# S4 with its two terms multiplied one by one and added in PSUM, for the first three sub-tiles

## The chip, the cores and the metric

The kernel runs on one core of a Trainium2 chip. The metric is the time of one execution on the device, in microseconds (us): the median of several runs.

## What is computed

The reference takes `x` of shape (32, 128, 64, 2): for each of 32 channels and 128 heads a row of 64 complex coefficients. Cut to what matters:

```python
dtA = (-exp(inv_A_real) + 1j * A_imag) * exp(log_dt)[:, None]     # (128 heads, 64)
Cc = B * C * (exp(dtA) - 1.0) / A
V = exp(dtA[:, :, None] * arange(1024))
h = 2.0 * einsum('chn,hnl->chl', Cc, V).real                      # S4: (32, 128, 1024)
h = h + einsum('bsi,oi->bso', layernorm(h), attn_weight) + attn_bias
n = layernorm(h)
gates = softmax(n @ Wr.T)
h = h + n @ W.T + b + sum_e 2.0 * gates[e] * (n @ A[e].T) @ Bm[e].T
```

So an S4 kernel matrix is built for each (channel, head), which gives 4096 tokens of 1024 values, and two 1024 x 1024 layers with a layer norm each follow; the second has a gated low-rank part.

## The kernel before, in words

The 4096 tokens are worked on in 32 sub-tiles of 128 tokens (4 heads of 32 channels). Two sub-tiles, i = 0 and 1, make a tile T (8 heads); there are 16 tiles. J = 2 * T + i numbers the sub-tiles.

**S4.** A position on the 1024 steps is split into a block a (8 of them, `KB`) and a step b (128). The real part over 64 complex coefficients is a contraction over 128 rows: 64 real and 64 imaginary. `make_u` (VectorE) multiplies `decay` by the sines in `turn` and gives `u`, a 128 x 128 matrix per head over the steps b. `make_m` (VectorE) gives the other operand, `m`, per head 8 blocks of 32 channels. It has two terms, because a complex product has two products: `x_t` part 0 times `q1` goes to `m`, `x_t` part 1 times `q2` goes to `m_im` (both L998), and the third instruction (L1001) adds `m_im` to `m`. All three are 128 x 1024 in fp32. `s4` (TensorE, L441) then takes for each block a and head q one product: `m[:, i, q, a*32:(a+1)*32]` is stationary (32 columns), `u` of the head is moving (128 columns), and the result goes to the 32 partitions q*32 of `ps_a`, columns a*128. The four heads of a block stand on the four column groups of the array. That is 32 products in each sub-tile; each shows as two matmuls and two weight loads in the profile.

**Behind S4.** `keep_h` (VectorE, L1007) reads `ps_a` when S4 is done, adds the bias into `h_tok` and sums for the mean; `square_1` (ScalarE, L683) sums the squares; `normalise_1` (VectorE, L1016 to L1032) makes `y` from `ps_a`; `high_1` (ScalarE, L703) and `low_1` (VectorE, L1038) split it into two fp16 halves in `x1_tok`, and SP's queue sends each through a DMA transpose (`turn_x1`). `attn` (TensorE, L449) takes 48 matmuls of 512 columns. `keep_h2` (VectorE, L1046), `square_2`, `normalise_2`, `high_2`, `low_2` and `turn_x2` do the same for the second layer; `project` (L497, L499) is its low-rank part and gate, `ffn_part` (L509) and `ffn_end` (L520) the layer, `finish` (L1108) the last addition.

**The prologue.** Ahead of the loop over the tiles the kernel also makes `q1`, `q2`, the first `u`, and turns and splits both weight matrices: the attention weight through TensorE (`turn_weight`, L487), then ScalarE (`wa_hi`, L728) and VectorE (`wa_lo`, L1149); the FFN weight through ScalarE (L739), VectorE (L1157) and DMA transposes (`turn_weights`). All of it is woven with the first three sub-tiles, (0,0), (0,1) and (1,0). The fourth, (1,1), is the first in the loop.

**What sets the order.** Each engine has its own list of calls, written out by hand, and runs it in that order; semaphores tie the lists together. For the change these matter: `s_terms` counts the two terms of `make_m`, `s_m` its sums, `s_s4` the finished S4 products, `s_h2` the `keep_h2`. `make_m` of the next sub-tile overwrites `m_im`. TensorE's list around the first two S4 is

```python
            turn_weight(1)
            pe.wait_ge(s_q, 2)
            s4(0, 0)
            square_ffn(KB + 2, KB + 4)
...
            attn_part(0, 0, range(0, 4), (0,))
            s4(0, 1)
            pe.wait_ge(s_wlo, low_done(5))
            turn_weight(7)
```

and for the third `ffn_part(0, 0, range(0, 3), (0,))` stands ahead of `s4(1, 0)`. On VectorE `make_m(0, 0)` is followed by `make_first_u(0)`, then `keep_h(0, 0)`, `attn_lo(0, 1)` and `normalise_1(0, 0)`; `make_m(0, 1)` by `attn_lo(5)`, `ffn_lo(8)`, `attn_lo(6)`, `keep_h(0, 1)`, `attn_lo(7)`; `make_m(1, 0)` by `keep_h2(0, 1)`, `make_u(1)`, the gate of (0,0) and `keep_h(1, 0)`.

Of the kernel before, what the change touches and what calls it, by code (L numbers as in the profile page):

```python
# [15 lines left out]
P = 128  # L16
C, H, N = 32, 128, 64
# [9 lines left out]
HS = P // C  # L27
# [21 lines left out]
BELOW_PI = 3.1415925  # L49
BELOW_TWO_PI = 6.283185  # L50
NA = KB + 2
PRE = EXPS + 40


def at_least(engine, semaphore, value):

    if isinstance(value, int) and value <= 0:
        return
    engine.wait_ge(semaphore, value)


def program(nc, x, log_dt, B, inv_A_real, A_imag, attn_w, attn_b, ffn_w, ffn_b, lora_a, lora_b,
            gate_w, out):
    with ExitStack() as ctx:
# [14 lines left out]
        steps_b = sb("steps_b", [P, P])  # L79
        steps_a = sb("steps_a", [P, NA])  # L80
        half_pi = sb("half_pi", [P, 1])
# [20 lines left out]
        m = sb("m", [P, SUB, HS, KB * C])  # L102
        m_im = sb("m_im", [P, HS, KB * C])
# [22 lines left out]
        turn, u = turn_u[:, 0, :, :], turn_u[:, 1, :, :]  # L126
# [14 lines left out]
        ps_a = ctx.enter_context(nc.psum_tensor("ps_a", [P, 2, HALF], F32))  # L141
# [48 lines left out]
        s_terms = sem("m_terms_ready")  # L190
        s_m = sem("m_ready")
        s_s4 = sem("s4_product_done")
# [72 lines left out]
        def scratch(where, *shape):  # L265
# [23 lines left out]
        ga, gb = scratch("y", 2, N), scratch("y", 2, N)  # L289
        ph, ph_k = scratch("x1_tok", NA, N), scratch("x1", NA, N)  # L290
        sc = turn_u[:, :, :, :].rearrange("p s a b -> p s (a b)")[:, :, 0:NA * N]\
            .rearrange("p s (a n) -> p s a n", n=N)
# [24 lines left out]
        def _(sp):  # L317
# [58 lines left out]
            for n in range(KB, 2 * KB):  # L376
                sp.dma_start(raw_block(n), ffn_rows[n - KB]).then_inc(s_wload[n], 16)
            sp.wait_ge(s_pre_dve, PRE)
            load_lora_a(wg_norm_rows, s_wgn)
# [39 lines left out]
        def _(pe):  # L419
# [11 lines left out]
            def s4(T, i):  # L431

                if isinstance(T, int) and (T, i) == (0, 0):
                    pe.wait_ge(s_u_0, 1)
                else:
                    pe.wait_ge(s_u, T + 1)
                pe.wait_ge(s_m, 2 * T + i + 1)
                at_least(pe, s_xn1, 2 * T + i)
                for a in range(KB):
                    for q in range(HS):  # L440
                        mm = pe.matmul(ps_a[q * C:(q + 1) * C, a // 4, (a % 4) * P:(a % 4 + 1) * P],  # L441
                                       m[:, i, q, a * C:(a + 1) * C], u[:, HS * i + q, :], start=True, stop=True)
                mm.then_inc(s_s4, 1)

            def attn_part(t, i, ks, halves=(0, 1), ps=ps_g1):
# [102 lines left out]
            pe.wait_ge(s_pre_act, 6)  # L548
            for first, dst, ready in ((0, ps_g1, PRE - 1), (N, ps_a, PRE)):
                pe.wait_ge(s_pre_dve, ready)  # L550
                for a in range(KB):
                    mm = pe.transpose(dst[:, a // 4, (a % 4) * P:(a % 4 + 1) * P], qn[:, a, first:first + 2 * N],
                                      ident[:, :])
# [78 lines left out]
            for o in range(2):  # L632
                cols = slice(o * HALF, (o + 1) * HALF)
                for k in range(KB):
                    if (o, k) == (0, 6):
                        turn_lora(t, 1)
                    for part, ws in ((0, wf_hi), (0, wf_lo), (1, wf_hi)):
                        pe.matmul(ps_g1[:, o, :], x2_part(1, part)[:, k, :], ws[:, k, cols],  # L638
                                  start=k == 0 and part == 0 and ws is wf_hi, stop=False)
# [211 lines left out]
        def _(pool):  # L851
# [3 lines left out]
                               pattern=[[-1, P]], channel_multiplier=1).then_inc(s_const, 1)  # L855
            pool.iota(steps_a[:, 2:NA], pattern=[[P, KB]], base=0, channel_multiplier=0,
                      allow_small_or_imprecise_dtypes=True).then_inc(s_const, 1)
# [13 lines left out]
        def _(dve):  # L871
# [11 lines left out]
            for tile, value in ((ones[:, :], 1.0), (half_pi[:, :], pi / 2), (quarter[0:N, :], 0.25),  # L883
                                (quarter[N:P, :], 0.0), (eps[:, :], EPS), (steps_a[:, 0:1], 0.5),
                                (steps_a[:, 1:2], 1.0)):
                last = dve.memset(tile, value)
# [11 lines left out]
            for k in range(6, 0, -1):  # L898
# [17 lines left out]
            tt(wexp, zr[:, 0:1, :].broadcast_to((P, KB, N)),  # L916
               steps_a[:, 2:NA].unsqueeze(2).broadcast_to((P, KB, N)), ALU.mult)
            tt(ph, zt[:, 0:1, :].broadcast_to((P, NA, N)), steps_a[:, :].unsqueeze(2).broadcast_to((P, NA, N)),
               ALU.mult)
# [38 lines left out]
            tt(qn[:, :, 2 * N:3 * N], wb[:, 1, :, :], wa[:, 0, :, :], ALU.subtract)  # L958
            assert done[0] == PRE

# [23 lines left out]
            def make_m(T, i):  # L984

                J = 2 * T + i
                dve.wait_ge(s_xt_sb, T + 1)
                at_least(dve, s_s4, J - 1)
                if isinstance(T, int):
                    at_least(dve, s_m, J)  # L990
                for part, dst in enumerate((m[:, i, :, :], m_im[:, :, :])):
                    c = x_t[:, part, i * P:(i + 1) * P].rearrange("p (h c) -> p h c", h=HS)\
                        .unsqueeze(2).broadcast_to((P, HS, KB, C))
                    f = (q1, q2)[part][:, :, columns(T, i)].rearrange("p a h -> p h a")\
                        .unsqueeze(3).broadcast_to((P, HS, KB, C))
                    if isinstance(T, int) and J == 0:
                        dve.wait_ge(s_q, part + 1)
                    dve.tensor_tensor(dst.rearrange("p h (a c) -> p h a c", a=KB), c, f, ALU.mult)\  # L998
                        .then_inc(s_terms, 1)
                dve.wait_ge(s_terms, 2 * J + 2)  # L1000
                dve.tensor_tensor(m[:, i, :, :], m[:, i, :, :], m_im[:, :, :], ALU.add).then_inc(s_m, 1)  # L1001

# [181 lines left out]
            round_turns(0)  # L1184
            dve.wait_ge(s_pre_dve, PRE)
            weight_norms(0, [whole(ps_g2)])
# [114 lines left out]
```

## Time and profile before

| | before |
|---|---|
| median of 3 runs | 840.18 us |
| lowest and highest | 838.75 and 841.95 us |
| the profiled execution, its own time | 838.85 us |
| its span, first to last instruction | 837.0 us |
| TensorE matmul busy | 811.0 us (97%) |
| VectorE busy | 586.9 us (70%) |
| ScalarE busy | 376.6 us (45%) |
| mean granted TensorE clock | 0.993 |

The profile is of one execution. Engines are PE (TensorE matmul), PEld (TensorE weight load), DVE (VectorE), ACT (ScalarE), POOL and SP (queues of DMA issues); L441 is line 441 of the kernel. Times are in us from the start of the span. "Idle before" is the time the engine did nothing ahead of an instruction, with what released it. The granted clock is 1.00 for 2.4 GHz and 0.50 for 1.2 GHz. The records of pipelined matmuls overlap: the busy time of a group is the time covered by at least one.

### The profile page before, as it was taken

How to read it: one execution, taken by the hardware profiler on the slowest of the kernel's cores; microseconds unless marked ns; L12 is line 12 of the kernel's file. 1: busy time of each engine (PE TensorE's matmuls, PEld its weight loads, DVE VectorE, ACT ScalarE, POOL GpSimd, SP SyncE). 2: the span in 40 equal slices, each digit the busy share in tenths (PEclk: the TensorE clock that was granted, in tenths of full speed). 3: DMA queues.
4: the chain of work that ended last, by engine and by line, in shares of the span. 5: the costliest groups of instructions: out<-in, count | busy, mean ns of one | idle time of the engine just before them, and what ended most of it. 6: DMA issues, size and time to landing. Idle time of an engine off the chain costs nothing.

```text
span 837.0 us, 16105 instructions
## 1 busy us (share of the span) xinstructions
PE 811.0 (97%) x6098; PEld 431.0 (51%) x6098; DVE 586.9 (70%) x1150; ACT 376.6 (45%) x747; POOL 3.0 (0%) x10
## 2 busy tenths in 40 slices
PE   6978799999999999999999999999999999999998
PEld 6854345545554555555545554555455555544543
DVE  6989786776758777675767677676867667577533
ACT  4767652625444352545445253545435254442210
POOL 0000000000000000000000000000000000000000
PEclk9999999999999999999999999999999999999999
DMA  7637644234323332333232323332233233323223
GB/s 267 193 71 136 131 88 77 67 71 87 75 51 73 65 87 52 86 76 76 62 75 63 75 63 75 84 78 51 65 74 83 55 88 75 71 54 67 59 51 76
DMA packets 175267, 68.47 MB, mean 82 GB/s; under 512 B 160456, under 2 KB 168776, under 8 KB 175248
## 3 DMA queue, kind: packets, MB, share of 16 engines
q1 hardware_dynamic: 175152, 68.09, 36.7%
q8 instruction: 11, 0.18, 0.1%
q10 hardware_dynamic: 96, 0.13, 0.0%
q14 instruction: 8, 0.07, 0.0%
HBM read 13.67 MB, written 16.78 MB: 36 GB/s over the span
## 4 chain that ended last, share of the span: by engine, by line
PE 88%; DVE 5%; issue 3%; ACT 2%; DMA 1%; SPq 0%; POOL 0%; POOLq 0%; ACTq 0%; DVEq 0%
PE ps_g L509 38%; PE ps_g L449 38%; PE ps_a L441 7%; PE ps_g L520 2%; PE ps_g L638 1%; PE ps_p L497 1%; PE ps_g L463 1%; PE ps_x L427 1%; DMA h_tok<-in_L_attn_weight 1%; PE ps_p L499 1%; DVE m L998 0%; DVE m_im L998 0%; PE ps_p L514 0%; ACT phase L657 0%; DVE wa_lo L1149 0%
## 5 line engine op out<-in xcount | busy, mean ns | idle before, releaser
L449 PE MATMUL ps_g<-wa_hi,x 128*128 128x512 f16 x1024 | 271.5, 381 | 2.9 <-DMA x<-x_tok 2.2
L509 PE MATMUL ps_g<-wf_hi,x 128*128 128x512 f16 x992 | 265.7, 381 | 1.1 <-DVE h_tok L1046 1.1
L449 PEld LDWEIGHTS ps_g<-wa_hi,x 128*128 128x128 f16 x1024 | 97.7, 98 | 123.4 <-issue 7.4
L449 PE MATMUL ps_g<-wa_lo,x 128*128 128x512 f16 x512 | 154.4, 381 | 0.0
L509 PEld LDWEIGHTS ps_g<-wf_hi,x 128*128 128x128 f16 x992 | 94.9, 98 | 108.0 <-issue 2.8
L509 PE MATMUL ps_g<-wf_lo,x 128*128 128x512 f16 x496 | 149.6, 381 | 0.0
L683 ACT ACTIVATE junk<-ps_a,stat 128x1024 bf16<-128x1024 f32 x32 | 35.6, 1113 | 147.4 <-DVE stat L1010 147.4
L1108 DVE SCALAR_TENSOR_TENSOR result<-ps_g,unscale,h_tok 128x1024 f32<-128x1024 f32 x31 | 39.8, 1283 | 72.0 <-PE ps_g L520 72.0
L703 ACT ACTIVATE x_tok<-y 128x1024 f16<-128x1024 f32 x32 | 33.8, 1057 | 123.4 <-DVE y L1032 123.4
L449 PEld LDWEIGHTS ps_g<-wa_lo,x 128*128 128x128 f16 x512 | 50.2, 98 | 60.7 <-issue 1.0
L509 PEld LDWEIGHTS ps_g<-wf_lo,x 128*128 128x128 f16 x496 | 48.5, 98 | 58.6 <-issue 0.6
L689 ACT ACTIVATE junk<-h_tok,stat 128x1024 bf16<-128x1024 f32 x32 | 36.7, 1147 | 91.0 <-DVE stat L1050 91.0
L441 PE MATMUL ps_a<-turn_u,m 128*32 128x128 f32 x2048 | 62.5, 274 | 2.4 <-DVE m L1001 2.1
L441 PEld LDWEIGHTS ps_a<-turn_u,m 128*32 128x32 f32 x2048 | 54.0, 110 | 10.8 <-issue 9.2
L1007 DVE SCALAR_TENSOR_TENSOR h_tok<-ps_a,bias_bc 128x1024 f32<-128x1024 f32 x32 | 39.2, 1223 | 24.7 <-PE ps_a L441 24.7
L1046 DVE SCALAR_TENSOR_TENSOR h_tok<-ps_g,unscale,h_tok 128x1024 f32<-128x1024 f32 x32 | 41.0, 1281 | 20.7 <-PE ps_g L449 20.7
L1038 DVE TENSOR_TENSOR x_tok<-y,x_tok 128x1024 f16<-128x1024 f32 x32 | 39.1, 1222 | 21.3 <-ACT x_tok L703 21.3
L709 ACT ACTIVATE stage<-xn 128x1024 f16<-128x1024 f32 x32 | 33.8, 1056 | 44.6 <-DVE xn L1057 44.6
L657 ACT ACTIVATE phase<-steps_b,quarter,z_turn 128x128 f32<-128x128 f32 x128 | 50.8, 479 | 0.0
L1063 DVE TENSOR_TENSOR stage<-xn,stage 128x1024 f16<-128x1024 f32 x32 | 39.2, 1225 | 11.4 <-ACT stage L709 11.4
L1032 DVE TENSOR_SCALAR y<-ps_a,stat 128x1024 f32<-128x1024 f32 x32 | 43.0, 1343 | 1.2
L998 DVE TENSOR_TENSOR m<-x_t,q 128x1024 f32<-128x1024 f32 x32 | 39.2, 1224 | 1.6
(188 smaller groups left out, 782.4 us busy)
## 6 DMA issues: line engine op xcount, KB each, us to landing
out<-result SPq DMA_DIRECT2D x124, 128.0 KB, 2.1
x_raw<-in_x SPq DMA_DIRECT2D x64, 64.0 KB
stage<-in_L_ffn_W SPq DMA_DIRECT2D x8, 512.0 KB, 9.8
h_tok<-in_L_attn_weight SPq DMA_DIRECT2D x2, 512.0 KB, 4.8
x<-in_L_attn_weight SPq DMA_DIRECT2D x2, 512.0 KB, 7.2
result<-in_L_attn_weight SPq DMA_DIRECT2D x2, 512.0 KB, 8.7
x<-x_tok SPq DMA_TRANSPOSE x64, 3.2
x<-stage SPq DMA_TRANSPOSE x64, 3.2
```

The source lines that it names most:

```text
L441: mm = pe.matmul(ps_a[q * C:(q + 1) * C, a // 4, (a % 4) * P:(a % 4 + 1) * P], m[:, i, q, a * C:(a + 1) * C], u[:, HS * i + q, :], start=T ...
L449: mm = pe.matmul(ps[:, o, :], x1_part(part, ps is ps_g2)[:, k, :], ws[:, k, o * HALF:(o + 1) * HALF], start=k == 0 and part == 0 and ws is ...
L509: pe.matmul(ps_g2[:, o, :], xs[:, k, :], ws[:, k, o * HALF:(o + 1) * HALF], start=k == 0 and xs is x2_hi and ws is wf_hi, stop=False)
L657: a = act.activation(phase[:, k, :], steps_b[:, :], ACT.Identity, scale=z_turn[:, bass.ds(T * HT + k, 1)], bias=quarter[:, :])
L689: act.activation(junk[:, :], h2_tok[:, i, :], ACT.Square, bias=stat_2[:, 1:2], accum_out=stat_2[:, 2:3]).then_inc(s_ssq2, 1)
L998: dve.tensor_tensor(dst.rearrange("p h (a c) -> p h a c", a=KB), c, f, ALU.mult)\
L1007: dve.scalar_tensor_tensor(out=h_tok[:, i, :], in0=whole(ps_a), scalar=1.0, in1=bias_bc[:, :], op0=ALU.mult, op1=ALU.add, accum_out=stat_1 ...
L1032: dve.tensor_scalar(y[:, :], whole(ps_a), stat_1[:, 1:2], stat_1[:, 7:8], ALU.add, ALU.mult).then_inc(s_xn1, 1)
L1038: dve.tensor_tensor(by_token(x1_tok[:, :], 1), y[:, :], by_token(x1_tok[:, :], 0), ALU.subtract)\
L1046: dve.scalar_tensor_tensor(out=h2_tok[:, i, :], in0=whole(ps), scalar=unscale[:, 0:1], in1=h_tok[:, i, :], op0=ALU.mult, op1=ALU.add, accu ...
L1063: dve.tensor_tensor(by_token(x2_tok, 1), xn[:, :], by_token(x2_tok, 0), ALU.subtract)\
L1108: dve.scalar_tensor_tensor(out=result[:, i, :], in0=whole(ps_g2), scalar=unscale[:, 1:2], in1=h2_tok[:, i, :], op0=ALU.mult, op1=ALU.add). ...
```

## The change

For J below `APART` = 3, `make_m` ends behind its two terms. `s4` waits for both (`s_terms`) and multiplies each with `u`: for each block a the four products with `m` (start of the PSUM group), then the four with `m_im` (its end). For all other sub-tiles nothing changes but the count in the waits on `s_m`, which has three sums fewer.

```diff
+APART = 3
@@ s4 (TensorE)
-                pe.wait_ge(s_m, 2 * T + i + 1)
+                if isinstance(T, int) and 2 * T + i < APART:
+                    pe.wait_ge(s_terms, 2 * (2 * T + i) + 2)
+                else:
+                    pe.wait_ge(s_m, 2 * T + i + 1 - APART)
                 at_least(pe, s_xn1, 2 * T + i)
+                terms = (m[:, i, :, :], m_im[:, :, :]) if isinstance(T, int) and 2 * T + i < APART else (m[:, i, :, :],)
                 for a in range(KB):
-                    for q in range(HS):
-                        mm = pe.matmul(ps_a[q * C:(q + 1) * C, a // 4, (a % 4) * P:(a % 4 + 1) * P],
-                                       m[:, i, q, a * C:(a + 1) * C], u[:, HS * i + q, :], start=True, stop=True)
+                    for term, last in zip(terms, (len(terms) == 1, True)):
+                        for q in range(HS):
+                            mm = pe.matmul(ps_a[q * C:(q + 1) * C, a // 4, (a % 4) * P:(a % 4 + 1) * P],
+                                           term[:, q, a * C:(a + 1) * C], u[:, HS * i + q, :],
+                                           start=term is terms[0], stop=last)
@@ make_m (VectorE)
                 if isinstance(T, int):
-                    at_least(dve, s_m, J)
+                    at_least(dve, s_m, J - APART)
+                    at_least(dve, s_s4, min(J, APART))
...
+                if isinstance(T, int) and 2 * T + i < APART:
+                    return
                 dve.wait_ge(s_terms, 2 * J + 2)
                 dve.tensor_tensor(m[:, i, :, :], m[:, i, :, :], m_im[:, :, :], ALU.add).then_inc(s_m, 1)
```

How the order of instructions changes is shown at two places. On TensorE, around the S4 of sub-tile (0,0), before (L487 is `turn_weight(1)`, L463 the squares of the FFN weight):

```order
L487 MATMUL ps_g<-ident,h_tok 128x128 x8
L441 MATMUL ps_a<-turn_u,m 32x128 x32
L463 MATMUL ps_x<-stage 128x128 x4
L463 MATMUL ps_p<-stage 128x128 x4
L463 MATMUL ps_x<-stage 128x128 x4
```

and with the change, whose lines are numbered 6 or 7 higher here (the pair of L447 rows stands eight times in all):

```order
L494 MATMUL ps_g<-ident,h_tok 128x128 x8
L447 MATMUL ps_a<-turn_u,m 32x128 x4
L447 MATMUL ps_a<-turn_u,m_im 32x128 x4
L447 MATMUL ps_a<-turn_u,m 32x128 x4
L447 MATMUL ps_a<-turn_u,m_im 32x128 x4
```

One row of 32 products has become 16 rows of 4, 64 products in all; the same stands at (0,1) and (1,0).

On VectorE, from `make_m(1, 0)` on, before (with the semaphores waited for):

```order
L998 TENSOR_TENSOR m<-x_t,q 128x1024 [waits m_ready,s4_product_done,x_transposed_copied]
L998 TENSOR_TENSOR m_im<-x_t,q 128x1024
L1001 TENSOR_TENSOR m<-m,m_im 128x1024 [waits m_terms_ready]
L1046 SCALAR_TENSOR_TENSOR h_tok,stat<-ps_g,unscale,h_tok 128x1024 [waits attn_product_done,first_ffn_rows_transposed]
L1050 TENSOR_SCALAR stat<-stat 128x1 [waits h2_ready]
```

and with the change:

```order
L1006 TENSOR_TENSOR m<-x_t,q 128x1024 [waits s4_product_done,x_transposed_copied]
L1006 TENSOR_TENSOR m_im<-x_t,q 128x1024
L1056 SCALAR_TENSOR_TENSOR h_tok,stat<-ps_g,unscale,h_tok 128x1024 [waits attn_product_done,first_ffn_rows_transposed]
L1060 TENSOR_SCALAR stat<-stat 128x1 [waits h2_ready]
L981 TENSOR_TENSOR turn_u<-decay,turn_u 128x1024 [waits s4_product_done,decay_ready,sines_ready]
```

The sum is gone, and `keep_h2(0, 1)` follows the second term directly. No other instruction moves on any engine, and SP's queue is the same.

## Rows read from the trace of the kernel before

**Rows 1.** The page, part 1, busy time of each engine.

```profile
PE 811.0 (97%) x6098; PEld 431.0 (51%) x6098; DVE 586.9 (70%) x1150; ACT 376.6 (45%) x747; POOL 3.0 (0%) x10
```

**Rows 2.** TensorE's waits from 105 us to the end.

```profile
PE ps_a L441 <- DVE m L1001: 2.1, 1, 2.1
```

**Rows 3.** The chain that ended last, 88 to 118 us: start, us, what.

```profile
88.07 3.74 PE ps_g L509 x9
...
105.37 1.95 PE ps_a L441 x64
107.32 10.47 PE ps_g L449 x48
```

**Rows 4.** Windows: stretch, its length, busy (instructions) of PE, PEld, DVE, ACT, POOL, granted clock, DMA, GB/s.

```profile
44.00:47.20 3.20, 0.00 (x0) 0.00 (x0) 3.20 (x4) 3.11 (x5) 0.00 (x0) 0.97 0.71 137
...
68.60:70.70 2.10, 0.00 (x0) 0.00 (x0) 2.02 (x2) 2.05 (x2) 0.00 (x0) 1.00 0.98 190
71.20:74.00 2.80, 2.80 (x8) 0.89 (x6) 2.73 (x10) 2.80 (x9) 0.00 (x0) 0.50 0.99 190
83.90:86.20 2.30, 0.00 (x0) 0.00 (x0) 2.27 (x3) 2.28 (x6) 0.00 (x0) 1.00 0.99 190
88.00:91.20 3.20, 3.13 (x8) 1.20 (x9) 2.08 (x7) 2.98 (x7) 0.00 (x0) 0.50 0.96 185
...
103.40:105.20 1.80, 0.00 (x0) 0.00 (x0) 1.76 (x3) 1.80 (x6) 0.00 (x0) 1.00 1.02 193
```

**Rows 5.** Timeline, first sub-tile: start, us, engine, line, operation.

```profile
32.41 1.23 DVE L1001 TENSOR_TENSOR m<-m,m_im 128x1024 f32<-128x1024 f32 x1
...
33.00 1.03 PE L487 MATMUL ps_g<-ident,h_tok 128*128 128x128 f32 x8
33.56 0.68 DVE L981 TENSOR_TENSOR turn_u<-decay,turn_u 128x512 f32<-128x512 f32 x1
...
34.34 1.95 PE L441 MATMUL ps_a<-turn_u,m 128*32 128x128 f32 x64 [0.31 <-issue]
...
36.42 1.22 DVE L1007 SCALAR_TENSOR_TENSOR h_tok<-ps_a,bias_bc 128x1024 f32<-128x1024 f32 x1 [0.58 <-PE ps_a L441]
```

**Rows 6.** The page, part 5, the S4 products and their loads.

```profile
L441 PE MATMUL ps_a<-turn_u,m 128*32 128x128 f32 x2048 | 62.5, 274 | 2.4 <-DVE m L1001 2.1
L441 PEld LDWEIGHTS ps_a<-turn_u,m 128*32 128x32 f32 x2048 | 54.0, 110 | 10.8 <-issue 9.2
```

**Rows 7.** Timeline, second sub-tile: start, us, engine, line, operation [idle before].

```profile
54.45 1.22 DVE L1001 TENSOR_TENSOR m<-m,m_im 128x1024 f32<-128x1024 f32 x1
...
55.83 1.96 PE L441 MATMUL ps_a<-turn_u,m 128*32 128x128 f32 x64
...
58.90 0.69 ACT L728 ACTIVATE wa_hi<-ps_x,scale 128x512 f16<-128x512 f32 x1 [3.35 <-PE ps_p L487]
...
59.31 1.21 DVE L1007 SCALAR_TENSOR_TENSOR h_tok<-ps_a,bias_bc 128x1024 f32<-128x1024 f32 x1
59.49 0.68 ACT L728 ACTIVATE wa_hi<-ps_p,scale 128x512 f16<-128x512 f32 x1
...
60.87 1.11 ACT L683 ACTIVATE junk<-ps_a,stat 128x1024 bf16<-128x1024 f32 x1 [0.70 <-DVE stat L1010]
```

**Rows 8.** Timeline, third sub-tile.

```profile
85.50 1.23 DVE L1001 TENSOR_TENSOR m<-m,m_im 128x1024 f32<-128x1024 f32 x1
...
86.50 1.06 ACT L677 ACTIVATE turn_u<-turn_u 128x1024 f32<-128x1024 f32 x1
...
86.64 1.28 DVE L1046 SCALAR_TENSOR_TENSOR h_tok<-ps_g,unscale,h_tok 128x1024 f32<-128x1024 f32 x1
...
86.75 0.18 PE L499 MATMUL ps_p<-wg,x 128*128 128x36 f16 x1
...
88.07 0.59 PE L509 MATMUL ps_g<-wf_hi,x 128*128 128x512 f16 x1 [1.14 <-DVE h_tok L1046]
...
93.76 1.23 DVE L1007 SCALAR_TENSOR_TENSOR h_tok<-ps_a,bias_bc 128x1024 f32<-128x1024 f32 x1 [1.77 <-PE ps_a L441]
```

## The prediction

> **What bounds the kernel now.** I read the page's busy shares first: TensorE is busy for 97% of the span, VectorE for 70% [rows 1]. A share over the whole span says little about a change that touches the first 105 us alone, so the next view is TensorE's waits. From 105 us to the end there is one, of 2.1 us, before S4 of the fourth sub-tile, for VectorE's sum of its `m` [rows 2]. Behind that product TensorE never waits again. So the kernel has two parts. From 105.37 us on [rows 3] it is a fixed stretch of TensorE work, and all before is a prologue whose length is the start of that S4. **What the change is worth is the shift of this one start.**
>
> In the prologue neither engine works alone. VectorE runs nearly without a break and feeds TensorE; TensorE stands idle in gaps (the windows show four without one matmul) [rows 4]. But at three places VectorE waits for TensorE, and these are the three S4 products of the change, because `keep_h` reads `ps_a` when S4 is done.
>
> **The price of one product and of one sum.** S4 of a sub-tile is 32 products, recorded as 64 matmuls, and takes 1.95 us [rows 5]. One matmul's record lasts 274 ns [rows 6], but four products run side by side on four column groups, so they follow each other every 30.5 ns. The second term adds 64 records: I take **+1.95 us for each of the three sub-tiles**. The sum that VectorE saves lasts 1.23 us and frees it 1.15 us earlier (32.41 to the next start, 33.56) [rows 5].
>
> The stationary operand is loaded twice as often, too. The 2048 loads last 110 ns each but take 54.0 us together [rows 6], 1.7 us for the 64 of a sub-tile, inside the products' 1.95. The Trainium skill speaks against this change here: "TensorE: Matmul & The Clock Gate", section Part 3 on packing small matmuls, has loads overlap matmuls in flight only where the row group differs, and here all loads use all 128 rows. By that rule the 64 added loads would lie bare, an estimate of 7 us for each sub-tile, and the sum below would come to about 19 us. The trace disagrees, and it decides.
>
> **First sub-tile (0,0).** TensorE ends `turn_weight(1)` at 34.03 and starts S4 at 34.34, released by `u`, which VectorE ends at 34.24 behind the sum [rows 5]. Without the sum `u` is there at 33.1, and TensorE itself is next: S4 starts 0.3 us earlier and ends 1.95 - 0.3 = 1.65 us later. `keep_h` (36.42) had waited for it already, so it goes 1.65 us later. Behind it on VectorE stand the `wa_lo` splits, `normalise_1` and `low_1`, behind S4 on TensorE the squares and `turn_weight(2)`; each feeds the other, and both are late by the same amount. VectorE then runs on without a long wait to the second sub-tile. **+1.6 us.**
>
> **Second sub-tile (0,1).** The sum ends at 55.67 and S4 starts at 55.83, straight behind TensorE's attention piece: its row shows no idle time ahead [rows 7]. So S4 gains nothing from the missing sum: the engine was not free. VectorE gets its three weight splits done 1.15 us sooner, and then waits in `keep_h` (59.31 before) for an S4 that ends 1.95 us later: `keep_h` itself goes some 0.55 us later. The larger delay runs past it. `turn_weight(7)` (L487) stands behind S4, ScalarE's two halves of `wa_hi` (58.90 to 60.17) wait for it, and `square_1` (60.87) stands behind them on ScalarE [rows 7]. They now end at 62.12, so `square_1`, with the whole normalisation, is 1.25 us later. **+1.2 us.**
>
> **Third sub-tile (1,0).** VectorE comes to it with no slack and goes from the sum (85.50) straight to `keep_h2` (86.64), for which TensorE's FFN piece waits until 88.07 [rows 8]. Without the sum that is 1.15 us sooner; the projection that ends at 86.93 (last matmul 86.75) then releases it, at about 86.95. So FFN and S4 start 1.1 us sooner. `make_u` must be ready: the sine it needs ends at 87.56, `u` then at 88.9, before the end of the FFN piece at 88.07 + 3.74 - 1.1 = 90.7 [rows 3]. S4 ends 1.95 - 1.1 = 0.85 us later, and `keep_h` (93.76), for which VectorE had already idled 1.77 us [rows 8], follows. From there to the fourth `m` it is a chain through `keep_h`, both normalisations and `low_1`. **+0.85 us.**
>
> SP's queue issues its transposes when the splits are ready, so they move with them; no DMA is added. The added semaphore waits cost nothing: for `m_im` VectorE waits for an S4 whose result its own `keep_h` has already waited for. The loop's code issues as many instructions as before. **Sum: 1.6 + 1.2 + 0.85 = +3.65 us.**
>
> **The clock** is the unknown term. TensorE is granted 0.50 (1.2 GHz) from 88.0 to 91.2, after two gaps in which it did almost nothing (2.3 us from 83.9, 1.1 us from 86.93 with the short projection between them) [rows 4, 8]. The nine FFN matmuls before the third S4 take 3.74 us there, where the 48 of the loop's attention take 10.47, or 0.218 us each [rows 3]; so the low level costs 3.74 - 1.96 = 1.8 us on the path. The change closes the second gap and leaves one of about 2.4 us. A gap of 2.1 us from 68.6 was followed by 0.50, one of 1.8 to 2.1 us before 105.37 was not [rows 4]. The bounds are -1.8 (the low stretch is gone) and +1.8 (another falls on the path, on a doubled S4, say). I take -0.5: the nearest rows say one and the other, and what is saved early can be lost again to another wait. **Total +3.15 us.** The profiled execution took 838.85 us, so it would take 842.0; the median of the runs, 840.18, is 1.33 above it, and the forecast is **843.3 us**, +0.37%, which is no change within the 0.5% (4.2 us) that a measurement of this kernel can tell.
>
> **Rival 1: the clock comes back.** The shortened gap no longer ends in the low level. The Trainium skill, same page, section Part 1 on the clock gate, states that activity releases the throttle and idle time brings it, which would favour this case. By rows it is 3.65 - 1.8 = +1.85, 842.0 us. For it: the second gap vanishes. Against it: the gap of 2.1 us at 68.6 fell.
>
> **Rival 2: the products hide.** TensorE has idle time in the prologue (gaps of 3.2, 2.1, 2.3 and 1.8 us) [rows 4], and if the second term lay in it, only VectorE's gains would be left: 0.3 at the first sub-tile, 0.7 at the second (`square_1` would follow `wa_hi` at 60.2 instead of 60.87) [rows 7], 1.1 at the third, about -2 in all and 838.2 us, still inside 0.5%. Against it: VectorE waits for S4 in two of three `keep_h`, with 0.58 and 1.77 us of idle time [rows 5, 8].
>
> **Rival 3: slower.** The two terms of one slice add into the same columns of `ps_a`, eight records or 0.24 us apart, while one record lasts 0.27 us. If the second must wait for the first to be through, S4 takes longer than twice 1.95 us. It decides from 0.35 us per sub-tile on (3 x 0.35 + 3.15 = 4.2). A stall of 0.06 us in each of 8 slices is 0.5 us, 1.5 in all: 844.8 us. With a further low stretch on the path it would be up to 846.6. Against it: the attention matmuls add into the same columns one straight after the other and keep their pace of 0.218 us at 0.38 us per record.
>
> **Rival 4: it does not do what it says.** The built program has the 64 products and no sum in exactly three places, so I leave this 1%.
>
> **Chances.** My sum with the low stretch in place 43%, rival 1 33%, rival 2 11%, rival 3 12%, rival 4 1%. Over 4.2 us slower come most of rival 3 and a quarter of the first case, whose 843.8 lies 0.5 below the limit: 20%. Faster than 836.0 is only a good run of rival 2 with the clock gained as well: 4%. The same: 76%. The range goes from rival 1 less the spread of the runs shown (838.75 to 841.95, so 1.5 to 1.8 on each side), 840.2, to rival 3 with half of its further low stretch, 845.9.
>
> **What the new profile would show.** S4 of the first three sub-tiles as 128 matmuls in 3.9 us; `keep_h` 1.6 us later at 38.1; `wa_hi` of block 7 near 62.5 (58.90 before); `keep_h2` of (0,1) near 88.4; the fourth S4 near 108.5, with TensorE waiting for the sum ahead of it and for nothing after it. I am wrong if a 128-record S4 lasts much over 3.9 us, if the shift at the fourth S4 isn't the shift of the end, or if the fourth S4 starts no later than 105.4.

## The result, and the profile after

| | before | with the change |
|---|---|---|
| median | 839.77 us (22 runs) | 841.87 us (22 runs) |
| lowest and highest | 836.33 and 841.95 us | 839.99 and 843.22 us |
| the profiled execution, its own time | 838.85 us | 842.04 us |
| its span | 837.0 us | 840.2 us |
| mean granted TensorE clock | 0.993 | 0.994 |

The ratio of the times is **1.0025, with a 95% interval of 1.0013 to 1.0036**: 2.1 us slower, which is no change within 0.5%. The forecast was 843.3 us and no change. Each kernel's runs spread over 3 to 6 us, more than the effect, so only many runs show its sign.

The page of the changed kernel, part 1, against [rows 1]:

```profile
PE 815.2 (97%) x6290; PEld 435.9 (52%) x6290; DVE 583.5 (69%) x1147; ACT 376.6 (45%) x747; POOL 3.0 (0%) x10
```

TensorE has 192 matmuls more and 4.2 us more busy time. VectorE has three instructions and 3.4 us less. The page's part 5, the S4 products with `m` and their loads, against [rows 6]:

```profile
L447 PE MATMUL ps_a<-turn_u,m 128*32 128x128 f32 x2048 | 66.4, 274 | 2.1 <-DVE m L1011 2.1
...
L447 PEld LDWEIGHTS ps_a<-turn_u,m 128*32 128x32 f32 x2048 | 54.4, 110 | 10.7 <-issue 9.1
```

TensorE's waits from 105 us to the end, as in [rows 2]: still one, of the same length, ahead of the fourth S4. The loop behind it is the same stretch as before.

```profile
PE ps_a L447 <- DVE m L1011: 2.1, 1, 2.1
```

The chain that ended last, 50 to 118 us (start, us, what), against [rows 3]:

```profile
52.38 1.97 PE ps_g L494 x8
54.35 3.36 PE ps_g L456 x12
57.71 3.63 PE ps_a L447 x128
...
89.08 0.19 PE ps_p L504
89.69 3.57 PE ps_g L516 x9
93.27 3.72 PE ps_a L447 x128
97.01 1.24 DVE h_tok L1017 x2
...
107.26 1.24 DVE m L1011
...
108.62 1.95 PE ps_a L447 x64
```

The second S4 and the third now take 3.63 and 3.72 us for 128 records, and both stand on the chain. The fourth S4 starts at 108.62 instead of 105.37, 3.25 us later, and the profiled execution is 3.19 us longer: the shift of this one start is the shift of the end.

Windows of the same trace (stretch, length, busy time and instructions of PE, PEld, DVE, ACT, POOL, granted clock, DMA, GB/s), against [rows 4]:

```profile
49.40:55.40 6.00, 4.81 (x19) 3.54 (x19) 5.62 (x11) 4.37 (x5) 0.72 (x1) 0.50 0.23 58
...
85.10:88.90 3.80, 0.00 (x0) 0.00 (x0) 3.80 (x5) 3.78 (x11) 0.00 (x0) 1.00 0.91 173
90.20:93.00 2.80, 2.80 (x8) 0.79 (x6) 1.89 (x5) 2.74 (x5) 0.00 (x0) 0.50 0.97 187
```

The two stretches in the low level both lie on the path here: one on the transposes of the attention weight and the attention products ahead of the second S4, one on the FFN products ahead of the third. The gap ahead of the FFN products has become one long one, 4.18 us up to the projection at 89.08.

Timeline of the changed kernel at the three places (start, us, engine, line, operation [idle before]), against [rows 5, 7, 8]:

```profile
31.65 0.68 DVE L988 TENSOR_TENSOR turn_u<-decay,turn_u 128x512 f32<-128x512 f32 x1
...
33.32 0.43 PE L447 MATMUL ps_a<-turn_u,m 128*32 128x128 f32 x8
...
33.56 0.40 PE L447 MATMUL ps_a<-turn_u,m_im 128*32 128x128 f32 x8
...
33.78 0.40 PE L447 MATMUL ps_a<-turn_u,m 128*32 128x128 f32 x8
...
37.16 1.22 DVE L1017 SCALAR_TENSOR_TENSOR h_tok<-ps_a,bias_bc 128x1024 f32<-128x1024 f32 x1 [3.22 <-PE ps_a L447]
...
61.41 1.23 DVE L1017 SCALAR_TENSOR_TENSOR h_tok<-ps_a,bias_bc 128x1024 f32<-128x1024 f32 x1 [3.11 <-PE ps_a L447]
...
63.62 1.11 ACT L690 ACTIVATE junk<-ps_a,stat 128x1024 bf16<-128x1024 f32 x1
...
87.00 1.22 DVE L1006 TENSOR_TENSOR m_im<-x_t,q 128x1024 f32<-128x1024 f32 x1
88.14 1.28 DVE L1056 SCALAR_TENSOR_TENSOR h_tok<-ps_g,unscale,h_tok 128x1024 f32<-128x1024 f32 x1
...
97.01 1.22 DVE L1017 SCALAR_TENSOR_TENSOR h_tok<-ps_a,bias_bc 128x1024 f32<-128x1024 f32 x1 [2.26 <-PE ps_a L447]
```

Eight records start every 0.22 us, whichever term they multiply. And where the sum stood, VectorE now waits: 3.22, 3.11 and 2.26 us ahead of the three `keep_h`, against 0.58, none and 1.77.

**How the shift grows.** The first `m` of a run starts between 28.5 and 30.0 us, with nothing of the change ahead of it (30.02 before, the latest of all traces, and 29.38 here). So I compare starts counted from it. The columns of the experiments below are read in the same way.

| start of | before | change | terms ×2, sums kept | no sums, one term |
|---|---|---|---|---|
| `keep_h` (0,0) | 36.42 | +1.38 | +1.75 | -0.36 |
| S4 (0,1) | 55.83 | +2.45 | +1.75 | +0.93 |
| `y` (0,1) | 63.60 | +3.39 | +2.69 | +0.13 |
| `keep_h2` (0,1) | 86.64 | +2.14 | +2.70 | -1.12 |
| FFN piece | 88.07 | +2.14 | +2.71 | -1.12 |
| `keep_h` (1,0) | 93.76 | +3.89 | +5.43 | -1.71 |
| fourth S4 | 105.37 | +3.89 | +5.43 | -1.71 |

In the change's column +1.38 is the first place. From +1.38 to +2.45 nothing of the change is at work: the 12 attention products ahead of the second S4 run in the low level and take 3.36 us, where the second kernel of the table takes 2.59. From S4 to `y` it is +0.94, the second place. Then -1.25 (the sum), +1.75 (the product) and -0.05 (the FFN products, which take 3.70 us from their first start at 89.57 instead of 3.74) make +0.5 at the third. **The three places cost 1.38 + 0.94 + 0.5 = 2.8 us, and the clock 1.1, against this one execution of the kernel before.**

The split hangs on that execution. Its low stretch there, 47.1 to 50.5 us, ended ahead of the attention products, so its second S4 came early. Three of the runs below have the lists of before up to that place: (1,0) alone, the unused products at the projection, and `keep_h2` moved alone. In all three a low stretch reaches into the attention products, and the second S4 starts 1.3, 2.0 and 1.1 us later than in the table's column. From S4 to `y` they take 6.97 us instead of 7.77. Here are S4 and `y` before, 7.77 us apart, and then in the run with unused products, 6.97 apart:

```profile
55.83 1.96 PE L441 MATMUL ps_a<-turn_u,m 128*32 128x128 f32 x64
63.60 1.34 DVE L1032 TENSOR_SCALAR y<-ps_a,stat 128x1024 f32<-128x1024 f32 x1
```

```profile
57.17 1.95 PE L441 MATMUL ps_a<-turn_u,m 128*32 128x128 f32 x64
64.14 1.34 DVE L1035 TENSOR_SCALAR y<-ps_a,stat 128x1024 f32<-128x1024 f32 x1
```

The change takes 8.71. So against an execution whose S4 is late too, the second product costs its full 1.74 us and the three places 3.6 in all. The `y` of those three runs is 0.3, 1.2 and 0.5 us later than before's (`keep_h2` alone, unused products, (1,0) alone), so against them the shift at `y` is 2.2 to 3.1 us instead of 3.39, and nothing of it is left for the clock.

### The profile page after: what moved, and what is told of

Read it like the earlier page. It is cut to its first block, busy times and chain, and to the rows that moved or that the text cites. A ratio compares the mean times of both kernels' runs of the same rounds, so it can differ in the third digit from the quotient of the medians.

```text
span 840.2 us, 16486 instructions
## 1 busy us (share of the span) xinstructions
PE 815.2 (97%) x6290; PEld 435.9 (52%) x6290; DVE 583.5 (69%) x1147; ACT 376.6 (45%) x747; POOL 3.0 (0%) x10
## 4 chain that ended last, share of the span: by engine, by line
PE 89%; DVE 5%; issue 3%; ACT 1%; DMA 1%; SPq 0%; POOL 0%; POOLq 0%; DVEq 0%; ACTq 0%
PE ps_g L456 38%; PE ps_g L516 37%; PE ps_a L447 7%; PE ps_g L527 2%; PE ps_g L645 1%; PE ps_p L504 1%; DVE params L885 1%; PE ps_x L428 1%; PE ps_p L506 1%; PE ps_p L521 0%; DMA x<-stage 0%; DVE y L885 0%; ACT phase L664 0%; DVE h_tok L885 0%; DMA params<-in_L_tok_B 0%
## 5 line engine op out<-in xcount | busy, mean ns | idle before, releaser
L447 PE MATMUL ps_a<-turn_u,m 128*32 128x128 f32 x2048 | 66.4, 274 | 2.1 <-DVE m L1011 2.1
L447 PEld LDWEIGHTS ps_a<-turn_u,m 128*32 128x32 f32 x2048 | 54.4, 110 | 10.7 <-issue 9.1
```

## Experiments

### The second product and the missing sum, each alone

With the sums kept (`make_m` is that of before), each product of the first three S4 is written twice; the lines are shown against the change's `s4`:

```diff
-                terms = (m[:, i, :, :], m_im[:, :, :]) if isinstance(T, int) and 2 * T + i < APART else (m[:, i, :, :],)
+                terms = (m[:, i, :, :],) * (2 if isinstance(T, int) and 2 * T + i < APART else 1)
...
-                                           start=term is terms[0], stop=last)
+                                           start=True, stop=True)
```

> The three sums stay on VectorE, and TensorE writes each of the 32 products of the first three S4 twice, to the same place (64 products, same result). Theory A (S4 is bare on the path at all three places, a second term costs 1.7 us each as the changed kernel's trace has it: 3.65 instead of 1.9 us): the fourth S4 starts about 5.2 us later against the prologue's own start than before, and the time is about 845 us, 0.6% over before. Rival B (the added products lie largely in TensorE's idle time and the change's loss has another cause): less than 1.5 us over before.

And the change with its sums left out, but its products with the first term alone, so that the second term's part of S4 is missing:

```diff
-                terms = (m[:, i, :, :], m_im[:, :, :]) if isinstance(T, int) and 2 * T + i < APART else (m[:, i, :, :],)
+                terms = (m[:, i, :, :],)
```

> The sums are left out, and S4 of the first three sub-tiles multiplies the first term only, 32 products (the second term's part of S4 is missing there, so the time is that of the change without its added products). Theory A: VectorE's 1.15 us are worth 0.3, 0.7 and 1.1 us at the three places, about 2 us in all, so 837.7 us, 0.25% under before. Rival C (the sums are on the path in full, as VectorE is the busy engine of the prologue): 3.5 us under before, 836.3 us.

The doubled products took 844.18 us, a ratio of 1.0062 (1.0040 to 1.0084): +5.2 us. The missing sums took 835.49 us, 0.9959 (0.9946 to 0.9973): -3.5 us. Together +1.7, close to the change's +2.1, so by the medians the two parts add. The chain with the doubled products:

```profile
53.72 2.59 PE ps_g L453 x12
56.31 3.63 PE ps_a L444 x128
...
89.44 4.00 PE ps_g L513 x9
93.43 4.39 PE ps_a L444 x128
...
109.46 1.95 PE ps_a L444 x64
```

and its first S4 alone, as a window on the matmuls into `ps_a` (busy PE, PEld, DVE, ACT, clock, DMA, GB/s):

```profile
32.90:36.60 3.70, 3.60 (x128) 3.46 (x128) 0.00 (x0) 0.00 (x0) 1.00 0.42 20
```

The second row of the chain settles the price of a product at the full clock. These products overwrite and never accumulate, and 128 records take 3.63 us, the same as with accumulation. So adding into the same columns costs nothing. 64 more records cost 3.63 - 1.95 = 1.7 us, not 1.95, since the last record's tail counts once. And the 128 loads take 3.46 us within the 3.60 of their products.

The table says where it lies bare: +1.75 at the first place (all of it), +0.94 at the second (against the early S4 of before), 1.75 at the third. There the low level adds to it: it reaches into the S4, whose 128 records take 4.39 us. Without the sums the steps are -0.36 at the first place and -1.25 at `keep_h2`: 1.6 us. At the second place the S4 came 0.93 late by a low stretch (47 to 54) and `y` followed 6.97 us behind it, as in the runs above that keep their sums, so nothing of it is the sum's. Another 0.6 comes up to the third `keep_h`, with no stretch in the low level ahead of the FFN piece. The 3.5 us of the medians is rival C's number, three full sums (3 x 1.15), and a miss for theory A's 2; but the trace shows 1.6 for the sums, and the rest goes with the clock: the twelve runs have a mean granted clock of 0.9948, the 30 of before beside them 0.9915.

### One sub-tile at a time

`APART` is replaced by a list, `SKIP = (0,)`, `(1,)` or `(2,)`, which names the sub-tiles that get two terms and no sum:

```diff
-APART = 3
+SKIP = (0,)
...
-                if isinstance(T, int) and 2 * T + i < APART:
+                if isinstance(T, int) and J in SKIP:
```

> The change for sub-tile (0,0) alone. Theory A: S4 starts 0.3 us sooner and ends 1.4 us later, everything behind goes 1.4 us later: 841.2 us. Rival B: no shift behind keep_h of (0,0).

> The change for sub-tile (0,1) alone. Theory A (S4 bare on the path behind both engines; the delay goes on through turn_weight(7), ScalarE's wa_hi and square_1): 1 us later at y of (0,1) and at the fourth S4, 0.1% over before. Rival D (S4 starts sooner when the sum is gone, so the loss is under 0.7 us): S4 starts before 55.0 us on the scale of the trace of before.

> The change for sub-tile (1,0) alone. Theory A: keep_h2 of (0,1) 1.15 us sooner, FFN and S4 1.1 us sooner, keep_h of (1,0) 0.6 us later: 840.4 us, within noise of before. If the low clock level no longer follows the shortened gap ahead of the FFN piece, 1.2 us sooner instead: 838.6 us. Rival B: faster by the full 1.1 us at the fourth S4 whatever the clock.

| | median, n = 12 | ratio | by the trace |
|---|---|---|---|
| (0,0) alone | 840.8 us | 1.0015 (0.9997 to 1.0033) | `keep_h` +1.38, fourth S4 +1.43 |
| (0,1) alone | 840.69 us | 1.0007 (0.9993 to 1.0020) | S4 to `y` 8.71 instead of 7.77 us |
| (1,0) alone | 838.94 us | 1.0000 (0.9983 to 1.0017) | `y` of (0,1) to `keep_h2` 21.79 instead of 23.04 us |

By the ratios they are +1.3, +0.6 and 0 us against before; their sum of 1.9 is near the change's 2.1. Each interval alone takes in 1, so the sum is no proof. At (0,1) the S4 started no sooner, as expected; in the profiled execution it started 2.2 us later, and the fourth S4 3.0 later, because the attention products ahead of it ran in a low stretch up to 56 us (3.93 us for the 12). On TensorE nothing that this kernel changes stands ahead of them. The same distance of 8.71 us stands with the sum kept and with the whole change: at this place the missing sum is worth nothing. Against the early S4 of before, 0.8 of the product's 1.75 hides, in slack that VectorE's weight splits leave: there `square_1` waited 0.70 us for `keep_h` [rows 7]. In the run with unused products, whose S4 came 2.0 us late, there is no such wait and the distance is 6.97 us, so 8.71 is that plus one product.

At (1,0) the trace has a surprise. Windows of that kernel:

```profile
83.20:85.50 2.30, 0.06 (x1) 0.00 (x0) 2.30 (x3) 2.28 (x6) 0.00 (x0) 1.00 0.97 190
86.20:88.20 2.00, 2.00 (x11) 0.74 (x9) 1.26 (x3) 1.98 (x2) 0.00 (x0) 1.00 1.00 195
```

A gap of 2.3 us, as long as the one of before [rows 4], is followed by products at 1.00.

### TensorE kept busy: is it the clock?

In the kernel before, ten products that nobody reads go ahead of the projection of (0,0):

```diff
+            pe.wait_ge(s_xt_sb, 2)
+            for _ in range(10):
+                pe.matmul(ps_x[:, :], wa_hi[:, 0, 0:P], wa_hi[:, 0, 0:HALF], start=True, stop=True)
             project(0, 0)
```

> The kernel before, with ten further matmuls of 512 columns (2.2 us at the full clock) into the unused ps_x in TensorE's gap ahead of the projection of (0,0); nothing reads their result. If the low clock level ahead of the third S4 comes from that gap and costs 1.2 to 1.8 us on the path: no stretch at 0.50 between 86 and 92 us, the nine FFN matmuls in 2.0 instead of 3.7 us, the fourth S4 and the time 1.2 us or more earlier, 0.15 to 0.2% under before. Rival E (the level is not from that gap, or the stretch is not on the path): the nine matmuls still take 3.7 us, or the fourth S4 does not move.

It took 837.48 us, 0.9977 (0.9960 to 0.9993); one of its 12 executions took 864.54 us and counts in the median alone. Its chain:

```profile
88.62 2.10 PE ps_g L509 x9
90.72 1.93 PE ps_a L441 x64
```

The nine FFN matmuls take 2.10 us instead of 3.74 [rows 3]. So the clock price of this place, forecast at 1.8 us, is 1.6, and products without any use win it back. The low level at 45 to 55.6 us stayed and made the second S4 2.0 us late in this run; `y` was late by 1.2 of it.

Then both kernels got these ten and 13 more ahead of `turn_weight(4)` (L487), so that they differ only in the change:

```diff
+            pe.wait_ge(s_xn1, 1)
+            for _ in range(13):
+                pe.matmul(ps_a[:, 0, :], wa_hi[:, 0, 0:P], wa_hi[:, 0:4, 0:P], start=True, stop=True)
             pe.wait_ge(s_wlo, low_done(3))
             turn_weight(4)
```

> The changed kernel with unused matmuls in both gaps (13 into ps_a ahead of turn_weight(4), 10 into ps_x ahead of the projection of (0,0)). With the clock at 1.00 throughout, what is left is the change's own work. Theory A: the fourth S4 is 2.9 us later than in the kernel before with the same fillers (1.4 + 0.9 + 0.6), and the time 840 us. Rival G (the loss is mainly the clock's doing): less than 1 us later than that kernel.

> The kernel before with the same fillers. Theory A: no stretch at 0.50 after 44 us that stands on the path; 1.5 to 2 us under before, 837.3 us, and 2.9 us under the changed kernel with fillers.

With the change 841.13 us, 1.0020 (1.0003 to 1.0036); without it 836.62 us, 0.9969 (0.9954 to 0.9984). Against each other the change costs 4.5 us here, more than the 2.1 in the bare kernels and than the 2.9 that was expected. Windows ahead of and in the FFN piece, with the change:

```profile
86.40:88.20 1.80, 0.00 (x0) 0.00 (x0) 1.80 (x2) 1.78 (x4) 0.00 (x0) 1.00 1.04 197
89.10:92.00 2.90, 2.90 (x8) 1.00 (x7) 1.90 (x5) 2.87 (x4) 0.00 (x0) 0.50 1.01 191
```

Without it, the window and then the chain:

```profile
86.20:87.20 1.00, 0.00 (x0) 0.00 (x0) 0.96 (x3) 0.98 (x2) 0.00 (x0) 1.00 1.10 204
```

```profile
87.27 2.10 PE ps_g L509 x9
89.37 1.93 PE ps_a L441 x64
...
102.93 1.95 PE ps_a L441 x64
```

With a gap of 1.1 us left the FFN piece ran at 1.00, with one of 1.9 us it ran at 0.50. So the pair is not the one I wanted, with the clock out of both; and a low stretch lies on the attention products ahead of the second S4 in both, from about 51 us on, in spite of the fillers. But the steps in the two traces refute the theory that the change's loss is the clock's doing. Between them the second S4 shifts by +1.18 (the first `keep_h` by +1.37), S4 to `y` grows by 1.74 (8.71 and 6.97 us), the missing sum gives 1.25 at `keep_h2`, and the product takes 1.74 at the third place: 3.4 us. The FFN piece adds 1.7 in the one alone (its nine matmuls take 2.10 us here and 3.79 there, from their first start at 88.80), and the fourth S4 is 5.1 us later. Rid of the low level ahead of the FFN, the kernel before gains 2.9 us, and the changed one, which isn't rid of it, nothing clear.

### A better place for the second product

The change issues the two terms by block, so even the first product waits for both. Here the 32 products with `m` go as soon as the first term is there, and those with `m_im` behind them; `u` is made between the two terms. TensorE's squares and its attention piece go behind S4. It is done for (0,0) and (0,1) only; (1,0) keeps its sum.

```diff
+                for n, term in enumerate((m[:, i, :, :], m_im[:, :, :]) if early else (m[:, i, :, :],)):
+                    if n:
+                        pe.wait_ge(s_terms, 2 * J + 2)
...
+                                           start=(n == 0 and a % 4 == 0) if early else True,
+                                           stop=(n == 1 and a % 4 == 3) if early else True)
@@ TensorE's list
-            square_ffn(KB, KB + 2)
+            square_ffn(KB, KB + 1)
...
-            square_ffn(KB + 2, KB + 4)
-            square_lora_a()
+            square_ffn(KB + 1, KB + 3)
...
             turn_weight(3)
+            square_ffn(KB + 3, KB + 4)
+            square_lora_a()
...
-            attn_part(0, 0, range(0, 4), (0,))
             s4(0, 1)
...
             turn_weight(7)
+            attn_part(0, 0, range(0, 4), (0,))
@@ VectorE's list
-            make_m(0, 0)
-            make_first_u(0)
+            make_m(0, 0, lambda: make_first_u(0))
```

> Two sub-tiles, (0,0) and (0,1), without the sum, but with all products of the first term issued as soon as that term is there and those of the second behind them, u of (0,0) made between the terms, S4 of (0,0) ahead of three of the four weight squares and S4 of (0,1) with turn_weight(7) ahead of the attention piece; (1,0) as before. Theory A says that the added 1.75 us can be hidden under VectorE's second term: keep_h of (0,0) 0.5 us and keep_h of (0,1) 1.7 us earlier than before, the fourth S4 about 1.7 us earlier, 0.2% under before. Rival F (the products hide nowhere, TensorE is the bound here): no earlier than before.

It took 839.35 us, 0.9990 (0.9975 to 1.0005): no difference from before, where 0.2% was expected. The steps came as expected: `keep_h` of (0,0) 0.40 sooner, `y` of (0,1) 1.83 sooner, and so on to the FFN piece. Then a stretch in the low level, 84.6 to 91.4 us, took 0.9 of it back: the nine FFN matmuls took 4.00 us and the third S4 2.55. The fourth `m` stood at -0.93, and the S4 behind it took 3.02 us in a further low stretch.

With one more move, `keep_h2(0, 1)` ahead of `make_m(1, 0)`, so that the FFN piece is released three VectorE instructions sooner:

```diff
-            make_m(1, 0)
             dve.wait_ge(s_wf_0, 32)
             keep_h2(0, 1, ps_g2)
+            make_m(1, 0)
```

> The same, with keep_h2 of (0,1) ahead of make_m of (1,0) on VectorE, so that the FFN piece need not wait for make_m; the sum of (1,0) stays. Theory A: FFN starts 1.1 us sooner than in the run without this reordering, the fourth S4 0.6 to 1.1 us sooner, 2.3 to 3 us (0.3%) under the kernel before. Rival: u of (1,0), made later now, holds S4 back and nothing is gained over the run without it.

and this move alone in the kernel before:

> The kernel before with one move: keep_h2 of (0,1) ahead of make_m of (1,0) on VectorE, no product added and no sum taken away. Theory A: FFN waits for the projection instead, 1.1 us sooner; with the fourth m behind the same chain the fourth S4 is 0.6 to 1.1 us sooner: 0.1% under before. If most of the gain of the full version comes from here, it is over 2 us.

Both together took **835.59 us, 0.9942 (0.9922 to 0.9961), 4.3 us faster than before**, and by the medians 6.3 faster than the change. Expected were 2.3 to 3 us. The move alone took 837.79 us, 0.9984 (0.9967 to 1.0001), an interval that takes in 1. Timeline of the first sub-tile with both:

```profile
29.61 1.23 DVE L1011 TENSOR_TENSOR m<-x_t,q 128x1024 f32<-128x1024 f32 x1
30.75 0.69 DVE L993 TENSOR_TENSOR turn_u<-decay,turn_u 128x512 f32<-128x512 f32 x1
31.35 1.22 DVE L1011 TENSOR_TENSOR m_im<-x_t,q 128x1024 f32<-128x1024 f32 x1
...
31.77 1.95 PE L450 MATMUL ps_a<-turn_u,m 128*32 128x128 f32 x64
...
33.54 1.93 PE L450 MATMUL ps_a<-turn_u,m_im 128*32 128x128 f32 x64
```

S4 starts 2.16 us earlier from the first `m` than before, and its first half lies beside the multiplication of the second term: that is how an added product hides. `keep_h2` (0,1) comes 3.22 us sooner, the FFN piece only 1.20, because the projection is next to hold it. The profiled execution of this kernel was its slowest, 838.92 us; the other five runs lie between 834.84 and 836.00. Its chain tells one reason:

```profile
86.61 3.64 PE ps_g L520 x9
90.25 1.93 PE ps_a L450 x64
...
103.81 3.53 PE ps_a L450 x64
```

The fourth S4 started 1.15 us sooner than before, counted from the first `m`, and then took 3.53 instead of 1.95 us, at the low level. The other five runs have no trace, but their mean granted clock is known: 0.995 and 0.996, against 0.990 in the profiled one and a mean of 0.9911 over the 29 runs of before beside them. The six have 0.9948 on the mean. That is 0.0037 of 840 us, by my estimate 3.1 us less lost to the low level, out of the 4.3 us gained; what is left is near the 1.15 of the trace. The first part alone gains 0.5 us at a mean clock of 0.9909, no more than before has, and the move alone 1.8 at 0.9930. So most of what the two gain together goes with the clock, not with the hidden product. That the reordering itself brings the higher clock is not shown.

The last run adds ten unused products at `project(0, 0)` and six at `turn_weight(4)` to that version:

> The full reordered version with unused matmuls of 512 columns in both gaps of TensorE (6 into ps_a ahead of turn_weight(4), 10 into ps_x ahead of the projection of (0,0)). If the low level is what is left to gain: no stretch at 0.50 ahead of the FFN piece, and 1 to 2 us under the full version, 834.5 us. Rival: the full version's gaps are short already and the added matmuls only delay what stands behind them: the same or slower.

It took 834.83 us, 0.9948 (0.9929 to 0.9967). Its fourth `m` starts 4.06 us sooner from the first one (1.13 without the fillers), and one stretch alone is at 0.50, 100.4 to 103.6, on the fourth S4, which takes 3.61 us. But the medians differ by 0.8 us (834.5 was expected) with overlapping intervals: the fillers change the profiled execution and the mean clock of the ten runs (0.9983), and not measurably the time.

## Why the prediction was right or wrong

**The bound and the metric of the shift: right.** The shift of the fourth S4 (3.25 us) is that of the profiled execution (3.19 us).

**The price of a product: mis-sized.** I multiplied 64 records by 1.95/64. A group that follows another has no tail of its own: 64 more records cost 1.7 us. On the three places, at 1.75 each in the trace, that is 0.6 us too much.

**The weight loads: right.** The window shows 3.46 us of loads inside 3.60 us of products, so the 19 us that I worked out against this did not come. (That sum put the 7 us of bare loads in place of each added product; with both it would have been 24.8.) The Trainium skill ("TensorE: Matmul & The Clock Gate", Part 3) lists loads as overlapping matmuls in flight only where the row group differs; the same section also names a background weight buffer as a second target that can be loaded ahead, which I left out. Here, at 192 added pairs, the loads lie beside the products, all with one row group; whether by the second target no run shows.

**First sub-tile: right, +1.38 for +1.65.** The sum's removal gave 0.37, the product 1.75.

**Second sub-tile: right in its path, +0.94 for +1.2** against the profile of before, and 1.74 against executions whose S4 is late. S4 gained nothing from the missing sum; the two halves of `wa_hi` and `square_1` behind `turn_weight(7)` moved as said. That `wa_hi` came at 62.46, forecast near 62.5, is luck in part: the low stretch ahead of S4 is in it, and so is the earlier first `m`.

**Third sub-tile: right in its path, +0.5 for +0.85.** `keep_h2` of (0,1) at 88.14, forecast 88.4. The sum gave 1.25 and the product took 1.75.

**The clock: wrong in its reason.** "The change closes the second gap and leaves one of about 2.4 us" is the step that failed. In the profile the two gaps became one of 4.2 us, up to the projection at 89.08. Before, the attention products at 71 to 74 ran in the low level [rows 4]; in the changed kernel they ran at 1.00 and were done earlier, while VectorE was late by 3.4 us, so TensorE had longer to wait. The low level came as before, and another stretch fell on the path ahead of the second S4. I took -0.5 us; the profiled execution had +1.1 ahead of the second S4 and -0.05 ahead of the third. That the forecast of its time was exact (842.0 for 842.04) is luck, errors that cancel: the steps were 0.85 too large, the clock 1.5 too small, and a first `m` that started 0.64 earlier made up the rest.

Over all runs the term was off the other way. For every execution of these two groups the mean granted clock is known. The 22 with the change have 0.9935 on the mean, the 92 of the kernel before that ran beside the experiments 0.9912. The difference is 0.0023 of 840 us: by my estimate the change's runs lose 1.9 us less to the low level. In the kernel before, time goes with this figure: ten runs at 0.994 took 836.2 to 837.0 us, 25 at 0.988 took 840.8 to 842.4. And at the same figure of 0.994 the 14 runs with the change took 840.0 to 842.5, by the medians 5.2 us more than those ten; at 0.992 it is 2.1 (5 runs against 21). So the clock term that fits the median is nearer -2 than -0.5. Why the changed kernel's runs have the higher clock is open, and where in them the low stretches fell no trace shows.

**Rival 1, the clock comes back: it did not** in the profiled execution (the FFN products took 3.70 us), though the kernel of (1,0) alone shows that it can. Over all runs it fits better than my sum: its +1.85 us lies inside the interval (1.1 to 3.0), my +3.15 just outside. With the unused products 3.74 us became 2.10. The Trainium skill's rule in Part 1 of the same page, activity releases and idle time throttles, agrees with that. The traces give no gap that decides it: 2.3 us was harmless once, 1.9 us was not.

**Rival 2, the products hide: refuted** as the change is written. One place of three hides 0.8 of 1.75 us, and that only where its S4 comes early. Written term by term, with TensorE's list reordered, it holds for the first two in the trace.

**Rival 3, a stall in accumulation: refuted.** 128 records take 3.63 us whether they add or overwrite.

**The size.** The medians say +2.1 us (1.1 to 3.0 by the interval), the parts alone 1.9 and 1.7. The steps without the clock are 2.8 against the one profile of before and 3.4 in the pair with unused products, where I had summed 3.65. I forecast +3.15. The mechanism of the three places held; the range and the verdict "no change" were wide enough for a clock term that was 1.5 us off. (The top of the range, rival 3 with half of its further low stretch, is 844.8 + 0.9 = 845.7 and not 845.9.) Only one execution of each kernel has a trace, so how the 2.1 us parts into work and clock stays an estimate. A low stretch can also begin, in one kernel, where TensorE had been idle for less than 1 us (45.7, in the version with both moves). Nothing here tells what decides it.

## What to carry to other kernels

Taking an operation from one engine and giving its work to another pays only the part by which the first was late at that place; price the added work in full wherever the consumer already waits for its producer, and read that from the idle time ahead of the consumer. An added product hides only if part of it can be issued while an operand that this part doesn't need is still being made, so split it by operand and move independent work behind it. Where a prologue feeds an engine that is full from then on, one start is the whole result: follow it place by place, and keep the clock in a sum of its own. One profile of the kernel before is one draw of that clock: look how other runs with the same list went up to the place, and put the mean granted clock of all runs beside their times before a gain or a loss is given to the work.

## What was not expected of the hardware

- S4 products in fp32, 32 stationary and 128 moving columns, four side by side on column groups, run at 0.22 us for eight records whether they overwrite or accumulate, with alternating terms, and with their loads (110 ns each) beside them: 3.46 us of loads in 3.60 us of products.
- The two levels of the clock fall differently in kernels that differ by little: the nine FFN matmuls took 2.10, 3.57, 3.64, 3.74 or 4.00 us on the chain. A 4.2 us gap, one of 1.9 us and one of 2.3 us were followed by 0.50; another of 2.3 us wasn't.
- Products without a use, 10 of 512 columns, made the kernel before 0.23% faster (0.9977, 0.9960 to 0.9993); with 13 more it was 0.31%.
